# Four block-matrix products of sequence 1 in two fp32r passes each, channel products in three steps, and a new order

## The reference

```python
x = x + ga * long_block(layernorm(x) * (1 + ca) + sa)
x = x + gb * moe(layernorm(x) * (1 + cb) + sb)
```

```python
h = layernorm(x);  x_conv = silu(causal_conv4(h))
q, k = l2norm(h @ Wq), l2norm(h @ Wk);  v = layernorm_per_head(h @ Wv)
u = sigmoid(x_conv @ Wig + big) * k * v
mem = scan: m[t] = gamma[t] * m[t-1] + u[t]
out = layernorm_per_head(mem) * q
out = group_norm_per_head(out) * sigmoid(x_conv @ Wog + bog)
h = x + out @ Wo
return h + silu(h2 @ Wgate) * (h2 @ Wval) @ Wout      # h2 = layernorm(h), 1024 wide
```

## Time and profile before

| | |
|---|---|
| three runs | 385.27, 385.52 and 614.99 us (one far off the other two) |
| median | 385.52 us |
| the profiled execution | 385.01 us, span 383.2 us |
| granted TensorE clock, mean | 0.993 |
| TensorE busy | 368.9 us, 1590 matmul entries |
| VectorE, ScalarE, GpSimd busy | 245.5, 200.2, 111.0 us |

### The profile page before, as it was taken

How to read it: one execution, slowest core, us unless ns; L and a number is a source line. 1 busy time by engine, 2 the same in 40 slices (tenths; PEclk the granted TensorE clock), 3 DMA queues, 4 the chain that set the end, 5 groups by cost and what they waited for, 6 DMA issues and landing times.

```text
span 383.2 us, 4573 instructions
## 1 busy us (share of the span) xinstructions
PE 368.9 (96%) x1590; PEld 286.2 (75%) x1590; DVE 245.5 (64%) x439; ACT 200.2 (52%) x314; POOL 111.0 (29%) x94
## 2 busy tenths in 40 slices
...
GB/s 222 362 31 42 50 109 62 2 0 0 9 131 2 0 41 3 44 164 71 137 85 152 193 97 96 97 126 134 126 98 96 96 102 129 45 70 149 125 85 55
DMA packets 18967, 34.81 MB, mean 91 GB/s; under 512 B 2528, under 2 KB 6496, under 8 KB 18944
## 3 DMA queue, kind: packets, MB, share of 16 engines
...
## 4 chain that ended last, share of the span: by engine, by line
PE 83%; DVE 7%; ACT 4%; DMA 2%; SPq 2%; issue 1%; POOL 0%; DVEq 0%; ACTq 0%
PE ps L1399 12%; PE ps L1401 12%; PE ps L1400 12%; PE ps L1432 6%; PE ps L1436 6%; PE ps L1433 6%; PE ps L1351 4%; PE ps L1356 4%; PE ps L1352 4%; PE ps L1117 3%; PE ps L1134 3%; PE ps L1118 3%; DMA w<-in_wsm 2%; DVE w L857 1%; PE ps L1303 1%
## 5 line engine op out<-in xcount | busy, mean ns | idle before, releaser
L372 POOL TENSOR_TENSOR wsm_lo<-w,wsm_hi 128x768 fp32r<-128x768 f32 (+1 forms) x40 | 71.2, 1784 | 204.1 <-ACT wsm_hi L694 183.2
L1399 PE MATMUL ps<-b_hi,wsm_hi 128*128 128x512 f32 x200 | 79.3, 396 | 0.0
L1401 PE MATMUL ps<-b_lo,wsm_hi 128*128 128x512 f32 x200 | 78.9, 395 | 0.0
L1400 PE MATMUL ps<-b_hi,wsm_lo 128*128 128x512 f32 x200 | 78.9, 395 | 0.0
L706 ACT ACTIVATE a_hi<-w 128x512 fp32r<-128x512 f32 x50 | 31.6, 632 | 86.4 <-DVE w L1060 83.5
L1056 DVE TENSOR_TENSOR w<-w,gate_b 128x512 f32<-128x512 f32 x44 | 43.1, 980 | 41.6 <-ACT w L700 41.6
L1065 DVE TENSOR_TENSOR a_lo<-w,a_hi 128x512 fp32r<-128x512 f32 x50 | 34.6, 693 | 31.6 <-ACT a_hi L706 31.5
L700 ACT ACTIVATE w<-ps 128x512 f32<-128x512 f32 x50 | 29.9, 597 | 34.7 <-PE ps L1401 34.6
L1399 PEld LDWEIGHTS ps<-b_hi,wsm_hi 128*128 128x128 f32 x200 | 37.7, 188 | 8.9 <-POOL wsm_lo L372 0.2
L1401 PEld LDWEIGHTS ps<-b_lo,wsm_hi 128*128 128x128 f32 x200 | 37.7, 188 | 8.9
L1400 PEld LDWEIGHTS ps<-b_hi,wsm_lo 128*128 128x128 f32 x200 | 37.7, 188 | 8.5
...
## 6 DMA issues: line engine op xcount, KB each, us to landing
...
```

What stands on the lines that cost most here:

```text
L372: return nc.gpsimd.tensor_tensor(lo, raw, f32(hi), ALU.subtract)
L1399: mm(bank, mgu(wsm_hi, slot, k, which), b_hi[b][:, k, :], start=k == 0, stop=False)
L1400: mm(bank, mgu(wsm_lo, slot, k, which), b_hi[b][:, k, :], start=False, stop=False)
L1401: last = mm(bank, mgu(wsm_hi, slot, k, which), b_lo[b][:, k, :], start=False, stop=k == KC - 1)
```

## The change

1. **Four of the six block-matrix products of sequence 1** (u, mem, oc, vo; not ssk and ssv, and none of sequence 0) run as `block_product`: each channel half has one fp32r pass for the high and one for the low part of the data. The matrices get no low part; GpSimd copies them to fp32r once (`matr`, `block_matrices`). New steps `bh.0` to `bh.3` on ScalarE write the high parts (for mem as a second square of the scan's result), new steps `bl.0` to `bl.3` on GpSimd write the low parts. These use `a_hi[1]`, `a_lo[1]`, `b_hi[1]`, `b_lo[1]`.
2. **`chan`**, the modulation products that give vectors by channel, is split into three steps; its readers wait for all three.
3. **Semaphores** of hn2 and hn3 are one (`hn23_ready`).
4. **All four tables** are new. On GpSimd the low part of chunk 4, which down.0.0 needs, stands behind bl.0, and that of chunk 5 behind bl.3.

```diff
--- before.py
+++ after.py
-    ones warm.2 scale shift.0 gate.0 shift.1 chan t1.0.0 t1.0.1 gate.1 q.0 qlo.0 k.0 klo.0 v.0 ig.0 iglo.0 ssk.0 ssv.0
...
+    ones warm.2 scale shift.0 gate.0 gate.1 chan.0 shift.1 t1.0.0 t1.0.1 chan.1 chan.2 k.0 q.0 klo.0 qlo.0 ig.0 iglo.0
+    ssk.0 v.0 ssv.0 ga.0 t1.1.2 u.0 og.0 mem.0 q.1 qlo.1 oc.0 k.1 klo.1 vo.0 v.1 wo.0 ig.1 tw.0 iglo.1 ga.1 ssk.1 t2.0
+    og.1 ssv.1 up.0.0 up.0.1 u.1 up.0.2 down.0.0 down.0.1 mem.1 down.0.2 up.0.3 up.0.4 oc.1 up.0.5 vo.1 down.0.3 up.0.6
...
+    silu.0.1 hid.0.0 og.1 hid.0.1 silu.0.2 sqm.1 bh.1 hid.0.2 rm.1 silu.0.3 bh.2 hid.0.3 silu.0.4 sqo.1 bh.3 hid.0.4
+    silu.0.5 ro.1 hid.0.5 gated.1 silu.0.6 wo.1 silu.0.7 hid.0.6 ehigh.0.0 hid.0.7 h2hi.1.0 h2hi.1.1 h2.1.0 h2.1.1
...
+        mats_r = sb("mats_r", [P, 2, P], FP32R)
...
+        BLOCKS = ["u", "mem", "oc", "vo"]
+
+        def block_in(name):
+            return {"u": W[1][3], "mem": W[1][5], "oc": W[1][3], "vo": W[1][6]}[name]
+
+        def block_parts(name):
+            return (b_hi[1], b_lo[1]) if name in ("u", "oc") else (a_hi[1], a_lo[1])
+
+        def blocks(name, c):
+            return KC * BLOCKS.index(name) + c + 1
...
+            def block_matrices():
+
+                pool.wait_ge(s("par_in"), 32)
+                nc.gpsimd.tensor_copy(mats_r[:, :, :], mats_sb[:, 1:3, :]).then_inc(s("block_lo"), 1)
+
+            def block_low(name):
+                for c in range(KC):
+                    pool.wait_ge(s("block_hi"), blocks(name, c))
+                    if name == "mem":
+                        pool.wait_ge(s("sqm_ready"), KC + c + 1)
+                    hi, lo = block_parts(name)
+                    low(lo[:, c, :], block_in(name)[:, c, :], hi[:, c, :]).then_inc(s("block_lo"), 1)
...
+            def block_high(name):
+                for c in range(KC):
+                    hi = block_parts(name)[0][:, c, :]
+                    if name == "u":
+                        act.wait_ge(s("og_psum"), KC * NB)
+                        act.wait_ge(s("u_ready"), KC + c + 1)
+                        ins = nc.scalar.activation(hi, W[1][3][:, c, :], ACT.Copy)
+                    if name == "mem":
+                        act.wait_ge(s("v_psum"), KC * NB)
+                        act.wait_ge(s("mem_ready"), KC + c + 1)
+                        ins = nc.scalar.activation(hi, PB(1)[:, c, :], ACT.Square)
+                    if name == "oc":
+                        act.wait_ge(s("uc_psum"), KC + c + 1)
+                        act.wait_ge(s("o1_ready"), KC + c + 1)
+                        ins = nc.scalar.activation(hi, W[1][3][:, c, :], ACT.Copy)
+                    if name == "vo":
+                        act.wait_ge(s("ssm_psum"), KC + c + 1)
+                        act.wait_ge(s("sqe_ready"), KC + c + 1)
+                        ins = nc.scalar.activation(hi, W[1][6][:, c, :], ACT.Copy)
+                    ins.then_inc(s("block_hi"), 1)
...
-                dve.wait_ge(s("mod_chan"), 1)
+                dve.wait_ge(s("mod_chan"), 3)
...
-            def chan():
-
-                pe.wait_ge(wmod_in[1], 16)
-                pe.wait_ge(wmod_in[2], 16)
+            def chan(i):
+
+                pe.wait_ge(wmod_in[1 if i == 0 else 2], 16)
                 pe.wait_ge(s("mod_gate_sb"), 1)
-                for j in range(3 * KC):
-                    part = wmod_raw[1][:, :, C + j * P:C + (j + 1) * P] if j < KC else \
+                for j in range(i * KC, (i + 1) * KC):
+                    part = wmod_raw[1][:, :, C + j * P:C + (j + 1) * P] if i == 0 else \
                         wmod_raw[2][:, :, (j - KC) * P:(j - KC + 1) * P]
                     for k in range(KC):
...
+            def block_product(name, out, matrix, ready):
+                hi, lo = block_parts(name)
+                for c in range(KC):
+                    pe.wait_ge(s("block_hi"), blocks(name, c))
+                    mm(out[:, c, :], matrix, hi[:, c, :], start=True, stop=False)
+                for c in range(KC):
+                    pe.wait_ge(s("block_lo"), 1 + blocks(name, c))
+                    mm(out[:, c, :], matrix, lo[:, c, :], start=False, stop=True).then_inc(s(ready), 1)
+
+            blk_r, cen_r = mats_r[:, 0, :], mats_r[:, 1, :]
...
             def u(b):
+                if b:
+                    pe.wait_ge(s("block_lo"), 1)
+                    block_product("u", PA(1), cen_r, "uc_psum")
+                    return
                 for c in range(KC):
                     pe.wait_ge(s("u_ready"), KC * b + c + 1)
                     mm(PA(b)[:, c, :], cen, W[b][3][:, c, :], start=True, stop=True).then_inc(s("uc_psum"), 1)
...
-                pe.wait_ge(s("hn3_ready"), b + 1)
+                pe.wait_ge(s("hn23_ready"), NB + b + 1)
```

More of the change, by code:

```diff
@@ L87 @@
+    wo.1 tw.1 up.0.7 down.0.4 down.0.5 t2.1 down.0.6 down.0.7 up.1.0 tm.0 up.1.1 up.1.2 down.1.0 down.1.1 up.1.3 up.1.4
+    t3.0 up.1.5 down.1.2 logits.0 down.1.3 up.1.6 wt.0 down.1.4 down.1.5 up.1.7 eup.0.0 eup.0.1 down.1.6 down.1.7
+    edown.0.0 tm.1 eup.0.2 eup.0.3 edown.0.1 edown.0.2 eup.0.4 eup.0.5 t3.1 edown.0.3 edown.0.4 eup.0.6 logits.1
+    eup.0.7 edown.0.5 edown.0.6 wt.1
 """
 SCALAR_PLAN = """
-    rstd.0.0.0 gate.0 rstd.0.0.1 rstd.0.1.0 shift.1 rstd.0.1.1 wsm.0 wsm.1 wsm.2 h1hi.0.0 h1hi.0.1 h1.0.0 h1.0.1 gate.1
@@ L91 @@
[L91 to L95, removed]
@@ L96 @@
-    ehigh.0.1 silu.1.7 ehigh.0.2 hid.1.7 acc.1 ehigh.0.3 esilu.0.0 ehid.0.0 esilu.0.1 ehid.0.1 esilu.0.2 ehid.0.2
-    ehigh.0.4 esilu.0.3 ehid.0.3 ehigh.0.5 esilu.0.4 ehigh.0.6 h3.1 esilu.0.5 esilu.0.6 ehid.0.4 ehigh.0.7 ehid.0.5
-    exp.1 ehid.0.6 esilu.0.7 ehigh.0.8 ehid.0.7 ehigh.0.9
+    rstd.0.0.0 rstd.0.0.1 gate.0 gate.1 rstd.0.1.0 rstd.0.1.1 wsm.0 wsm.1 h1hi.0.0 h1.0.0 shift.1 h1hi.0.1 wsm.2 h1.0.1
+    wsm.3 wsm.4 xconv.0 q.0 sqk.0 ig.0 rk.0 sqv.0 wsm.5 rv.0 ga.0 h1hi.1.0 h1hi.1.1 h1.1.0 h1.1.1 sqm.0 og.0 rm.0 q.1
@@ L99 @@
+    esilu.0.2 ehigh.0.4 ehid.0.1 esilu.0.3 ehid.0.2 ehigh.0.5 esilu.0.4 ehid.0.3 esilu.0.5 ehigh.0.6 ehid.0.4 h3.1
+    ehigh.0.7 esilu.0.6 ehigh.0.8 ehid.0.5 exp.1 ehid.0.6 esilu.0.7 ehid.0.7 ehigh.0.9
 """
 VECTOR_PLAN = """
-    var0.0.0 var0.0.1 scaled0.0.1 scaled0.0.0 shifted.0.0 var1.0.0 shifted.0.1 var1.0.1 scaled hn1.0.0 hn1.0.1 vsum
-    modc var0.1.2 h1lo.0.0 h1lo.0.1 conv.0.0 conv.0.1 xlo.0.0 xlo.0.1 scaled0.1.2 shifted.1.2 var1.1.2 a1.0 uk.0
-    hn1.1.2 uv.0 gamma.0 mem.0 conv.1.0 h1lo.1.0 h1lo.1.1 osig.0 o1.0 conv.1.1 sqe.0 gbc gated.0 outlo.0 xlo.1.0
@@ L105 @@
[L105 to L109, removed]
@@ L110 @@
-    plus_x.1 var3.1 elo.0.2 egated.0.3 hn3.1 elo.0.3 egated.0.4 egated.0.5 elo.0.4 egated.0.6 lgsub.1 h3lo.1 elo.0.5
-    elo.0.6 topk.1 egated.0.7 wt.1 elo.0.7
+    var0.0.0 var0.0.1 scaled0.0.0 scaled0.0.1 shifted.0.0 shifted.0.1 var1.0.0 var1.0.1 hn1.0.0 hn1.0.1 var0.1.2 vsum
+    h1lo.0.0 modc conv.0.0 h1lo.0.1 conv.0.1 xlo.0.0 scaled scaled0.1.2 xlo.0.1 shifted.1.2 var1.1.2 modg.0 hn1.1.2
+    a1.0 uk.0 uv.0 gamma.0 mem.0 h1lo.1.0 conv.1.0 h1lo.1.1 o1.0 sqe.0 osig.0 conv.1.1 gated.0 gbc outlo.0 xlo.1.0
```

54 lines of the change are left out of this document (35 added, 19 removed).

## The result

The changed kernel took 391.77 us in the median (389.88 to 395.45), 1.0147 times the kernel before on the same chip (95% interval 1.0107 to 1.0187), some 5.7 us slower. The forecast was 386.8, its range ended at 390.4. The profiled execution took 394.49 us, span 392.6; it is the second longest of its six, so I read from it where the time lies and take the size from the medians.

A forecast was written before the change was run, and what follows sets the result against it. TensorE's own work was taken to bound the kernel from 83 us, ScalarE from 28 to 41 us. Terms -3.2 - 1.1 + 0.2 + 5.6 = +1.5 on 385.01 gave 386.5, raised toward the runs' median to 386.8 us; range 382.2 to 390.4.

The forecast's parts named there:

- part 3: Front up to wo.0, paced by ScalarE: h1hi.1.0 0.3 to 0.4 us later, chain onward unchanged, wo.0 0.2 us later.
- Rival B: GpSimd and VectorE block each other, decided at hidlo.0.0 near 86.4 us; slower, 390.9 us; chance 0.14.
- Part 1: Four block products on TensorE after 82 us, each as four 0.232 us passes, give back 3.2 us.
- Part 2: Waits that go: u.1's 0.8 us and oc.1's 0.3 us, together 1.1 us gained.
- Part 4: New TensorE waits for the split's ScalarE and GpSimd work, from up.0.1 to the wt steps: 5.6 us lost.
- Rival A: The new order covers the split's chains; only up.0.1's wait and some 0.3 us remain; 382.4 to 383; chance 0.30.
- The sum behind t2.0: Forecast difference from TensorE's t2.0 transposes to the end of the kernel: +1.3 us.

The follow-up runs named there:

- e6: Changed kernel with gbc moved between o1.0 and sqe.0 on VectorE, where GpSimd is idle; 387.01 us, ratio 1.0031.
- e12: Changed kernel with gbc left in place and GpSimd's squares sqk.1 and sqv.1 moved behind chunkhi.4; 386.79 us, ratio 1.0018.
- e7: As e6, but all four block products are single fp32 products again, GpSimd's order kept by waits; 387.31 us, ratio 1.0043.
- e15: As e7, all four products in fp32, with u.1 moved back ahead of up.0.1; 386.72 us, ratio 1.0035.
- e13: As e9, but u.1 is one fp32 product in its old place, chunk.4 held in its place by a wait; 387.84 us, ratio 1.0044.
- e11: As e6, but u.1 (old place) and vo.1 are single fp32 products, chunk.4 moved behind bl.1 on GpSimd; 394.27 us, ratio 1.0198.
- e9: As e6, all four products split, with down.0.3 moved ahead of vo.1 on TensorE; 386.42 us, ratio 1.0005.

## Why the prediction was wrong, point by point

- **The step that failed** stands in part 3: "The chain onward (sqm, rm, o1, oc, vo, ro, gated, wo.0) has the same members", with all further moves of VectorE's table costed at nothing. The chain had a new member, gbc, between gated.0 and outlo.0; and there it stood under GpSimd's subtractions and multiplications. The term is +5.5 to +5.9 us instead of 0 (18.08 against e6's 12.60 and before's 12.17), 3.0 of it the stop and most of the rest the clock behind it, for which the prediction had no price either. e6 and e12 show it by taking it out: 387.0 and 386.8 us.
- **Rival B had the mechanism and the wrong place.** I looked for the collision in the stage where the change adds work to GpSimd (hidlo.0.0, at 94.83 us in the changed kernel, took 0.73 us; a later hidlo, at 100.92, took 1.79; TensorE waited for neither), priced it at one GpSimd instruction, and admitted only operations with two SBUF inputs. It struck where work was moved, cost what was left of one GpSimd instruction and three whole ones for four dependent operations, and two of the four had one input. That B's 390.9 us lies near the measured 391.8 is luck: it was added up from hidlo.0.0, sqe.1 and the two wt, for none of which TensorE waited.
- **Part 1, the products:** right in size. u.1 stands as four passes in 0.93 us (the changed kernel, TensorE):

```profile
94.88 0.63 PE L1333 MATMUL ps<-b_hi,mats_r 128*128 128x512 f32 x2
95.34 0.62 PE L1336 MATMUL ps<-b_lo,mats_r 128*128 128x512 f32 x2
95.81 0.39 PE L1423 MATMUL ps<-b_hi,wff_hi 128*128 128x512 f32 x1
```

- **Part 2:** right, u.1 and oc.1 wait no more.
- **Part 3, the front up to h1hi.1.0:** the order is right to a few tenths (in e7 the silu of half 1 starts at 25.58, 1.2 us earlier, h1hi.1.0 at 41.26, wo.0 at 61.74; said were 1.0 earlier, 41.0 to 41.4, 61.8). In the changed kernel's own profile h1hi.1.0 came at 43.72. What I had not seen is that the front hangs on when the gate's weights land. TensorE's gate product began between 9.62 and 11.99 us in 17 profiles; among those with the changed kernel's front order wo.0 came at 60.91 where it began at 9.87 (e15), at 65.74 where it began at 11.35 (e13), at 64.88 where it began at 11.99 (e11). The clock has a part in it: e6 and e9, alike up to there, began at 10.96 and 10.93 behind stops of 2.40 and 2.51 us, but the granted clock of 12 to 16 us was 1.00 in e6 and 0.64 in e9, and wo.0 came at 62.52 and 63.78. The changed kernel's own profile is of the late kind (11.13, wo.0 +2.6). How often that falls in the timed runs no trace shows; its +2.6 is not a cost of the change that I could show.
- **Part 4, the waits:** 4.5 us for 5.6, each of the named places but wt there. up.0.1 1.36 (said 1.4), mem.1 0.24 (0.4), up.0.4 0.19 (0.5), vo.1 1.76 (1.0), tw.1 0.5 (1.0), t2.1 0.43 (0.7), wt 0 (0.6); up.0.1 and t2.1 are the idle times of the rows, the others are read from the distances of passes. The prediction's own terms for mem.1 (6.8 against 6.3) give 0.5, not its 0.4. Rival A is out. The two largest:

```profile
92.02 0.47 PE L1423 MATMUL ps<-b_hi,wff_hi 128*128 128x512 f32 x1 [1.36 <-ACT w L696]
...
115.90 0.51 PE L1336 MATMUL ps<-a_lo,mats_r 128*128 128x512 f32 x1 [1.17 <-POOL a_lo L384]
```

- **The sum behind t2.0:** +1.3 said, +0.9 measured. Of the 3.2 us of the split 2.3 did not arrive (e6 against e7). Parts 1, 2 and 4 as measured give +0.2; the 0.7 left I could not place.

No version here beats the kernel before; the best, e9, is level with it.
